# Attention over blocked edges: the next row's loads issued one per group of the row, in the order of need

## The reference

```python
for i in range(L):                      # L = 4
    Q = _ln(h @ Wq[i], gq[i], bq[i])
    K = _ln(h @ Wk[i], gk[i], bk[i])
    qi = Q[src]
    kj = K[dst]
    score = (qi * kj).sum(-1) + 0.1 * (edge_attr * qi[:, :RBF]).sum(-1) + logm[dst]
    smax = jax.ops.segment_max(score, src, num_segments=N)
    es = jnp.exp(jnp.minimum(score - smax[src], 20.0))
    denom = jax.ops.segment_sum(es, src, num_segments=N)
    alpha = es / (denom[src] + 1e-10)
    m = h[dst] @ Wm[i]
    aggi = jax.ops.segment_sum(alpha[:, None] * m, src, num_segments=N)
    z = jnp.concatenate([h, aggi], axis=-1) @ Wu[i]
    z = jnp.where(z > 0, z, 0.01 * z)
    h = _ln(h + z, go[i], bo[i])
```

## Time and profile before

| | us |
|---|---|
| median of three runs | 9781.21 |
| lowest, highest | 9767.11, 9783.75 |
| the profiled execution | 9751.35 |
| its span, from first to last instruction | 9749.5 |
| PE busy, share of the span | 7941.9 (81%) |
| DVE busy | 6192.3 (64%) |
| ACT busy | 5099.4 (52%) |
| POOL busy | 6259.4 (64%) |
| mean granted TensorE clock | 0.882 |

### The profile page before, as it was taken

The page is one execution under the profiler, slowest core; times in us unless marked ns, Lnnn a source line. Parts: engine busy times, 40 slices in busy tenths (PEclk is TensorE's granted clock), DMA queues, the critical chain, the costliest instruction groups (busy, mean ns, idle before and its releaser), DMA issues. The chain is left out here.

```text
span 9749.5 us, 371154 instructions
## 1 busy us (share of the span) xinstructions
PE 7941.9 (81%) x155829; PEld 7354.9 (75%) x155829; DVE 6192.3 (64%) x15990; ACT 5099.4 (52%) x15175; POOL 6259.4 (64%) x7533
## 2 busy tenths in 40 slices
PE   6376676667658888888689988999799979997999
PEld 6255555555547777777679987998799969996999
DVE  6365555555547777777777767776777767774111
ACT  0122222222237777777567776777577757773000
POOL 2277777777766666666568766777587748772000
PEclk9677777777779999999789988999799979997999
DMA  9721212121135555555356645665466636663655
GB/s 286 235 49 43 49 43 49 43 49 43 43 107 176 178 175 177 175 175 177 106 192 222 216 156 171 216 218 181 136 218 218 210 103 220 214 218 142 253 244 214
DMA packets 736824, 1544.96 MB, mean 158 GB/s; under 512 B 159232, under 2 KB 462632, under 8 KB 724399
## 3 DMA queue, kind: packets, MB, share of 16 engines
q1 hardware_dynamic: 631057, 1443.17, 44.1%
q0 software_dynamic: 103968, 77.87, 3.9%
q10 hardware_dynamic: 126, 0.03, 0.0%
HBM read 1101.49 MB, written 417.51 MB: 156 GB/s over the span
## 5 line engine op out<-in xcount | busy, mean ns | idle before, releaser
L801 POOL DMA_INDIRECT edge_records<-rec_space,slot_i x1600 | 1901.7, 1189 | 768.8 <-issue 768.8
L1774 ACT ACTIVATE vals<-carry_h,weight 128x49 f32<-128x49 f32 x9604 | 2320.5, 326 | 6.4
L1611 PE MATMUL psum<-TT,hd_t 128*128 128x97 bf16 x28812 | 1527.4, 209 | 147.8 <-DMA hs_t<-one_hots 110.6
L1611 PEld LDWEIGHTS psum<-TT,hd_t 128*128 128x128 fp8e4 x28812 | 1365.8, 99 | 162.7 <-issue 160.0
L1819 POOL TENSOR_TENSOR vals<-vals 128x343 f32<-128x343 f32 x1372 | 1041.9, 759 | 92.9
L744 ACT COPY one_bsT<-psum 49x500 f32<-49x500 f32 x400 | 207.9, 568 | 1641.9 <-PE psum L727 1641.9
L1814 POOL TENSOR_TENSOR vals<-vals 128x343 f32<-128x343 f32 x1372 | 1042.3, 760 | 4.7 <-ACT vals L1774 4.7
L723 PE MATMUL psum<-ident,key 125*125 125x125 bf16 x1600 | 351.1, 307 | 822.3 <-DVE base L775 704.3
L1614 PE MATMUL psum<-ts,hs_t 128*128 128x49 bf16 x28812 | 977.7, 185 | 21.4 <-issue 20.4
L1679 DVE SCALAR_TENSOR_TENSOR xks<-recs,psum 128x343 f32<-128x343 f32 x1372 | 695.7, 507 | 441.2 <-PE psum L1614 432.2
L723 PEld LDWEIGHTS psum<-ident,key 125*125 125x125 bf16 x1600 | 320.1, 215 | 849.9 <-issue 849.9
(11 more groups left out here) (331 smaller groups left out, 17712.8 us busy)
## 6 DMA issues: line engine op xcount, KB each, us to landing
AJ<-adjacency SPq DMA_DIRECT2D x35, 5488.0 KB, 16.6
recs<-attributes SPq DMA_DIRECT2D x196, 686.0 KB, 5.7
hs<-one_hots SPq DMA_DIRECT2D x392, 336.0 KB, 3.0
one_hots<-hots SPq DMA_DIRECT2D x343, 336.0 KB, 5.2
edge_records<-zeros SPq DMA_DIRECT2D x49, 2278.5 KB, 22.8
recs_g<-edge_records SPq DMA_DIRECT2D x49, 2278.5 KB, 9.7
recs<-attributes SPq DMA_DIRECT2D x196, 514.5 KB, 3.7
hd_t<-one_hots SPq DMA_DIRECT2D x196, 448.0 KB, 4.5
```

Of the source, the lines that this page charges most:

```text
L801: e.indirect_dma_start(REC[:, :], bass.IndirectOffsetOnAxis(ap=slot_i[:, i % 4, s:s + 1], axis=0), rec_out[:, (i // 2) % 4, s, i % 2, :], ...
L1611: e.matmul(D(g, c), hd_t[:, p, g, c, :], TD[:, k, g * GC + c, :], start=k == 0, stop=k == 2)
L1774: last = e.activation(vals[:, c, 0, :], carry_h[:, par(back), c, :], ACT.Copy, scale=weight[:, par(back), c:c + 1])
```

## The change

The eight steps of SP become ten, with waits between them. `behind(g)` waits until DVE has done the first operation (L1679) of g groups of the present row. `next_sources` is split into its halves, with the slots apart, and the last two steps change places.

```diff
-                    def next_sources():
+                    def next_sources(h):
                         if ahead:
                             e.wait_ge(max_gathered.sem, nth(max_gathered, 1, 1))
-                            for h in range(2):
-                                load_hots(b + 1, hs_t[:, q], 0, s_src[q][h], half[h])
+                            load_hots(b + 1, hs_t[:, q], 0, s_src[q][h], half[h])
+
+                    def next_slots():
+                        if ahead:
                             load_slots(b + 1, q)
+
+                    def behind(g):
+                        if ahead:
+                            e.wait_ge(dve_link.sem, nth(dve_link, g))
...
                     hot(2, 1)
+                    behind(1)
                     next_targets(0)
                     next_recs(0)
+                    behind(4)
                     next_targets(1)
+                    behind(5)
                     hot(0)
-                    next_sources()
+                    next_sources(0)
+                    behind(6)
+                    next_sources(1)
+                    next_slots()
+                    behind(NG)
+                    next_recs(1)
                     hot(1)
-                    next_recs(1)
```

## The result

| | before | after |
|---|---|---|
| median, us | 9778.99 (4 runs, 9767.11 to 9783.75) | 10086.1 (4 runs, 10065.87 to 10120.24) |
| profiled execution: span, us | 9749.5 | 10075.0 |
| ratio after / before | | 1.0319, 95% interval 1.0288 to 1.0351 |

The changed kernel is 3.2% slower. Ahead of the first pass the two programs are the same, and yet the first attention row begins at 4933.0 instead of 4911.7 us: 21 of the 325.5 us are of that stretch, in which executions of the same instructions differed by as much in other runs (4911.1 to 4938.0). Nearly all the rest, 290 us, lies in the rows of the passes.

The account below looks back on a forecast made before the run. PE was taken to set the pace in the four attention passes. Late hs +250, issue gaps -35 and hs_t +5 gave +220 us, 10000 us on the median, 2.2% slower; range for 8 of 10: 9840 to 10110 us.

Parts of the forecast that it names:

- The step that carried it: SP's queue lands in issue order, so hs groups 3 to 5 behind recs reach PE's second L1628 block late.
- The term: PE's wait for hs groups 3 to 5 in the passes: 1.3 us a row, 192 rows, +250 us.
- The allowance for rows in which recs runs fast: Best-case row with 0.2 us to spare and no wait; ends 0 and 1.9 us, 1.3 us taken.
- The load-by-load list: Effect of each changed SP load: hs_t's second half and slots nothing, recs and hs groups 3 to 5 the cost.
- The gaps given back: PE's issue gaps in the passes, read as late instruction fetches: a quarter of 132.6 us off, -35 us.
- hs_t: PE's waits on hs_t's first half, 0.4 us to spare: +5 us, bounds -22 and +77 us.
- The mechanism named for it: hd_t's second half goes 2.3 us later and its 448 KB end shortly before hs's, closer ahead of hs_t.
- the sum: 250 - 35 + 5 = +220 us on the span of 9749.5 us; 10000 us on the median, 2.2% slower.
- The rival on the other side: Bursts go, nothing is late: 22 us on hs_t and half the issue gaps go, 9693 us; 9%.
- The signs named beforehand: Profile after: PE waits on hs, two hs landing times, recs 4.5 us, issue gaps 90 to 110, row 1.1 us longer.
- the signs of being wrong: PE's hs wait under 60 us, hs_t waits up over 80 us, or rows longer with no DMA named.
- the narrower one of 9920 to 10080: Range in us given to the forecast itself, with a 60% chance.

Follow-up runs that it names:

- Cuts alone: The changed kernel with recs and hs groups 3 to 5 back in the old order, all other new waits kept: 9685.25 us, ratio 0.9893.
- a stand alone: The kernel before, with hs groups 3 to 5 held back until DVE's first group of the next row, recs behind: 9986.67 us, ratio 1.0204.
- half of recs ahead: The changed kernel with recs' second half cut in two 343 KB loads, one ahead of hs groups 3 to 5, one behind: 9782.71 us, ratio 0.9998.
- hs late: hs groups 3 to 5 held until DVE's first group of the next row, recs behind: kernel before, 9986.67 us; changed kernel, 9912.82 us.
- the two slowest: Changed kernel, slots moved to the row using them: 10151.81 us; kernel before with exchange, hs_t's second half and slots held back: 10201.55 us.

## Why the prediction was right, and where it was not

**The step that carried it was right.** The queue lands in the order of issue, so hs behind recs is late. With all but the exchange kept, the loss turns into a gain, which shows that this step is the cause. The term was +250 us, 1.3 us a row. Measured in the changed kernel: 333 us in 186 of 192 rows, 1.8 us each; in the rows of the stretches the gaps before the slots blocks go from 14.8 to 323.1 us, +308. The allowance for rows in which recs runs fast was too large. Some luck is in it that the term came this near. It was read from rows of the old bursts, and there, with the exchange alone, the wait is 195.6 us, 1.0 us a row. The load-by-load list puts the holding back of hs_t's second half and slots at nothing; beside the exchange it isn't nothing, since with it the wait before the slots blocks is 423.6 us instead of 195.6.

**The gaps given back** were -35 in the sum, and are -107 in the rows of the stretches (113.9 to 6.4 us outside the slots blocks). Cuts alone take 74 of the 115.6 us, a stand alone 33. I had given the cuts a chance only inside a rival. The Trainium skill (Runtime: NRT & Kernel Launch, section Instruction fetch mechanics) has the crossing of instruction blocks mostly hidden. In the rows of the kernel before, 113.9 us of 3423.5, 3%, are gaps that end 1.2 to 1.65 us after an instruction packet: the trace agrees with "mostly", and these 3% are what the cuts could win.

**hs_t** was +5 and is +21 (110.6 to 131.4 us). The mechanism named for it fits: hd_t's second half, held back alone and with it closer ahead of hs_t, makes 67 us inside the passes, and with hs moved behind hs_t these waits all but go.

**What was missing is the clock.** PE's instructions took 74 us longer, and the sum had no term for it. For the rows of the stretches the account is 308 - 107 + 21 + 74, less 6 us of waits on other engines and small gaps: +290, where the sum had 250 - 35 + 5 = +220. The misses of the first two terms, +58 and -72, nearly cancel, which is luck; that leaves the clock as about the whole distance between the forecast of 10000 and the 10086 measured. The 10086 lies inside the range of 9840 to 10110, and 6 us above the narrower one of 9920 to 10080 that the forecast itself had.

**The rival on the other side** said that with nothing late the cuts would give 9693 us, by 22 us of hs_t and half of the issue gaps. As a forecast for the changed kernel it was wrong, since h1, hs groups 3 to 5, was late in nearly every row. The cuts gave 9685 us once the exchange was taken out, and half of the gaps did go; but the waits on hs_t grew by 19 us, and 38 us came from PE's shorter busy time, which the rival did not have, so that its number is in part luck. That this gain stood in a rival and not in the sum's main line, where it applies as well, is the error behind the second term.

**The signs named beforehand.** A wait before the second slots block in some 190 rows and of 200 to 300 us: 186 and 333, named issue instead of DMA hs. Two kinds of landing for hs of 336 KB, near 3 and near 5.5 us: 3.9 and 5.8. recs in 4.5 us: 5.3, wrong. Issue gaps of 90 to 110: 6, wrong. A row 1.1 us longer: 290 / 192 = 1.5. Of the signs of being wrong, two came by the letter: the waits that the profile gives to DMA hs stayed at 5.7 us, under 60, and the rows lengthened with no DMA named. Only the landing times show that it was the load all the same, and not something on DVE or POOL.

## What to carry to other kernels

Where loads land in the order of issue, as here, each load delays all behind it. So rank the loads of a steady loop by how much time each has to spare between its landing and its use, and count the bytes ahead of each. In the row followed here, recs landed at 6566.1 and DVE used it at 6569.86, nearly 4 us later; hs groups 3 to 5 had 1 us. The largest load, with the time to spare, should not go ahead of the one without. Cutting bursts of loads can pay even where no load is late: here 115.6 us of gaps were PE waiting for its instructions, and the cuts alone left 41.3. A change that mixes both should be taken apart: here one part was worth -1.1% and the other +4.1% on top of it.

DVE's use of that recs load, the first group of its half in the next row, in the kernel before:

```profile
6569.86 0.51 DVE L1679 SCALAR_TENSOR_TENSOR xks<-recs,psum 128x343 f32<-128x343 f32 x1 [0.94 <-PE psum L1614]
```

## What the hardware showed that I had not expected

- PE's granted clock fell after long single stands. Over whole passes it was 0.99 before and with 118 to 267 us of standing (half of recs ahead; hs late), 0.97 to 0.98 in the run with the exchange alone (196 us), 0.96 in the changed kernel (333 us), 0.94 with 375 us and 0.93 with 424 us; PE's busy time for the same instructions went from 3262 to 3412 us. The total of standing doesn't order these runs: 267 us left the clock alone, 196 us lowered it. The number of long gaps does. PE had 19 gaps of 1.5 us and more in the rows before, 21 to 31 in the runs with half of recs ahead or hs late, 61 with the exchange alone, 116 in the changed kernel, 124 and 168 in the two slowest. In the changed kernel 63 of the 73 gaps of 2 us and more had a stretch at the lower clock begin by 4 us after their end, and 2 of the 129 under 1.5 us. One such gap in the changed kernel, PE first, then 2 us at half the clock and, later, 2 us at the full one (columns as in the stretches above). The gathers of a group take 1.88 us there, elsewhere in the row 1.09:

```profile
6613.06 0.44 PE L1641 MATMUL psum<-slots,neg_ident 128*128 128x504 bf16 x1 [2.59 <-issue]
...
6613.90 1.88 PE L1624 MATMUL psum<-TT,hd_t 128*128 128x97 bf16 x21
```
```profile
6614.00:6616.00 2.00, 2.00 (x33) 2.00 (x31) 1.61 (x3) 0.00 (x0) 0.65 (x1) 0.50 0.03 8
6618.00:6620.00 2.00, 2.00 (x58) 2.00 (x56) 1.59 (x5) 1.39 (x7) 1.07 (x4) 1.00 0.85 239
```

- The price of one exchange depended on its surroundings by a factor of four and more: +1.0% in the old row, +4.1% (10086.1 against 9685.25) in the cut one, +5.4% (1.0463 against 0.9930) with hs_t and slots alone held back.
- Waits on a DMA's semaphore that lasted 1.8 us were put down to "issue" by the profile. Two kinds of wait hid under that word, and the trace tells them apart by what ended just before: the landing of hs 0.09 us before PE started, or an instruction packet 1.2 to 1.65 us before.
